# Output projection, second norm and gate logits: from single items among the score work to one TensorE piece per tile ahead of a value block

## What is computed

```
mod = silu(c) @ wmod                                   # six rows of 256 per batch
h = layernorm(x) * (1 + ca) + sa
x1 = x + ga * (softmax(causal(rope(q) @ rope(k).T / 4)) @ v  @ out_w + out_b)    # 16 heads of 16
h2 = layernorm(x1) * (1 + cb) + sb
logits = h2 @ gate_w.T;  top 4 of 16 experts (2 of 4 groups), weights from sigmoid(logits)
out = x1 + gb * (sum over the 4 experts of w * expert(h2) + shared(h2))          # SwiGLU, width 192
```

## Time and profile before

| | us |
|---|---|
| three runs, lowest / median / highest | 3317.51 / 3322.41 / 3326.74 |
| profiled execution: own time / span of the instructions | 3325.06 / 3323.3 |
| mean granted TensorE clock | 0.946 |
| first exponential of attention / end of the last one | 344 / 2234 |

### The profile page before, as it was taken

The page is one execution under the profiler, slowest core; times in us unless marked ns, Lnnn a source line. Parts: engine busy times, 40 slices in busy tenths (PEclk is TensorE's granted clock), DMA queues, the critical chain, the costliest instruction groups (busy, mean ns, idle before and its releaser), DMA issues.

```text
span 3323.3 us, 61013 instructions
## 1 busy us (share of the span) xinstructions
PE 2940.9 (88%) x22500; PEld 1617.6 (49%) x22500; DVE 2242.5 (67%) x5047; ACT 1782.1 (54%) x2736; POOL 1316.6 (40%) x1685
## 2 busy tenths in 40 slices
PE   7888699999999999899989878788877899999886
PEld 4433133334333334333333222227867788999775
DVE  7787398888888888999978656313921125555455
ACT  3322457666566665566555445565644555666222
POOL 6855111224422245221357556343045523441355
PEclk9989799999999999999989888899988999999898
DMA  4833513222322223212324433144355545664455
GB/s 163 207 108 94 113 40 63 61 66 67 86 62 54 54 69 102 49 31 60 76 92 125 108 88 95 54 135 140 93 166 164 169 136 163 178 183 139 143 175 152
DMA packets 290690, 359.05 MB, mean 108 GB/s; under 512 B 65404, under 2 KB 243212, under 8 KB 290140
## 3 DMA queue, kind: packets, MB, share of 16 engines
q1 hardware_dynamic: 259516, 279.94, 31.1%
q0 software_dynamic: 30208, 71.87, 7.2%
q10 hardware_dynamic: 672, 3.34, 0.4%
HBM read 206.25 MB, written 139.21 MB: 104 GB/s over the span
## 4 chain that ended last, share of the span: by engine, by line
PE 54%; DVE 11%; ACT 10%; issue 7%; another core or an unknown queue 3%; POOL 2%; DMA 1%; SPq 1%; DVEq 0%; ACTq 0%; POOLq 0%
PE PB L1140 13%; ACT P L1616 9%; PE PB L1067 9%; PE PB L1156 9%; DVE mx L1435 7%; PE PB L1014 6%; PE PB L1037 6%; PE PB L1050 5%; PE PB L1125 2%; PE PB L1081 2%; PE PB L1104 1%; POOL x_slots L1811 1%; PE PB L1017 0%; POOL P L1763 0%
## 5 line engine op out<-in xcount | busy, mean ns | idle before, releaser
L1435 DVE TENSOR_REDUCE mx<-PB 128x1 f32<-128x512 f32 (+3 forms) x2560 | 1405.7, 603 | 289.8 <-PE PB L1014 145.3
L1616 ACT ACTIVATE P<-PB 128x1024 f32<-128x1024 f32 (+3 forms) x1280 | 1100.0, 894 | 747.9 <-PE PB L1050 705.3
L1014 PE MATMUL PB<-KO,QO 64*128 64x512 bf16 (+3 forms) x2560 | 775.1, 358 | 80.9 <-DVE mx L1435 54.5
L1067 PE MATMUL PB<-P,V 128*17 128x512 f32 (+3 forms) x5120 | 610.5, 549 | 15.8 <-POOL P L1763 15.8
L1037 PE MATMUL PB<-QO,KO 64*128 64x512 bf16 (+3 forms) x2560 | 547.9, 358 | 56.4 <-ACT P L1616 30.6
L1050 PE MATMUL PB<-QO,KO 34*128 34x512 bf16 (+3 forms) x2560 | 539.0, 356 | 47.7 <-remote 38.3
L1014 PEld LDWEIGHTS PB<-KO,QO 64*128 64x128 bf16 x2560 | 203.8, 94 | 761.6 <-DVE mx L1435 542.7
L1546 DVE TENSOR_TENSOR haT<-sl,PB 64x128 f32<-64x128 f32 x350 | 101.5, 290 | 559.6 <-ACT sl L1695 383.2
L1140 PE MATMUL PB<-xT,ws 128*128 128x128 f32 x3432 | 446.6, 281 | 16.3 <-issue 9.6
L1763 POOL TENSOR_SCALAR_AFFINE_SELECT P<-P 128x256 f32<-128x256 f32 x512 | 207.5, 415 | 601.6 <-ACT P L1616 597.4
L1140 PEld LDWEIGHTS PB<-xT,ws 128*128 128x128 f32 x3432 | 420.3, 198 | 20.5 <-issue 11.7
(11 more groups left out here) (179 smaller groups left out, 3317.0 us busy)
## 6 DMA issues: line engine op xcount, KB each, us to landing
xq<-x_slots SPq DMA_DIRECT2D x286, 128.0 KB
qk_parts<-pt SPq DMA_DIRECT2D x192, 128.0 KB, 2.4
KO<-qk_parts SPq DMA_DIRECT2D x192, 128.0 KB, 3.9
y_slots<-yo SPq DMA_DIRECT2D x191, 128.0 KB
QO<-qk_parts SPq DMA_DIRECT2D x64, 256.0 KB, 3.6
rden<-rden_rows SPq DMA_DIRECT2D x256, 64.0 KB
y_slots<-mx SPq DMA_DIRECT2D x95, 128.0 KB
v_rows<-vst SPq DMA_DIRECT2D x16, 544.0 KB, 3.4
```

The source lines that it names most:

```text
L1014: mm = pe.matmul(PB[:, bank, 0:n], QO[half, k3, j, 128 * t:128 * t + 128], KO[half, k3, j, 512 * kc:512 * kc + n], start=True, stop=True)
L1067: mm = pe.matmul(PB[32 * j:32 * j + 17, 7, c0:512], V[:, g % 2, kt, 17 * j:17 * j + 17], P[:, pbuf(g, i, j // 2), j % 2, 0:n], start=kt == ...
L1435: dve.tensor_reduce(mx[:, j, t, kc:kc + 1], PB[:, u.bank[item], 0:n], AX.X, ALU.max).then_inc(s["mx"], 1)
L1616: act.activation(P[:, pbuf(g, i, p), :, 0:n], PB[:, 2 * p:2 * p + 2, 0:n], ACT.Exp, scale=0.25).then_inc(s["exp"], 1)
```

## The change

The tile's three TensorE parts (`o_logits` of tile it - 6, `o_turn` of tile it - 5, `o_proj` of tile it - 1) stand one behind another, ahead of the value block of a step. VectorE's parts of logits and projection become items of their own, `x_logits` and `x_proj`, placed right behind the three, ahead of the value block too. `o_h2` and `o_stat` follow in the same step, behind the exponential; `o_x1` and `o_load` at the same place of the next step. The rates count tiles: 0.3 a step in g % 4 == 3 (after a lead of 1), 0.48 in the two groups after it; a tile takes two steps at least, and credit goes on growing while a projection waits for "packed". In the expert stage the generator is pumped as before, five yields a job, but a tile has three yields now and had up to seven.

```diff
     def project(b):
-        stages = ("o_load", "o_proj", "o_x1", "o_stat", "o_h2", "o_turn", "o_logits")
-        for it in range(16 + len(stages) - 1):
-            for d in reversed(range(len(stages))):
+
+        for it in range(16 + 6):
+            while it - 1 in range(16) and not o.has("packed", b, 3, (it - 1) // 4):
+                yield "wait"
+            for d, name in ((6, "o_logits"), (5, "o_turn"), (1, "o_proj")):
                 if 0 <= it - d < 16:
-                    while stages[d] == "o_proj" and not o.has("packed", b, 3, (it - d) // 4):
-                        yield
-                    unit(stages[d], b, it - d)
-                    yield
+                    unit(name, b, it - d)
+            for d, name in ((6, "x_logits"), (1, "x_proj")):
+                if 0 <= it - d < 16:
+                    o(name, b, it - d)
+            yield "pe"
+            for d, name in ((4, "o_h2"), (3, "o_stat")):
+                if 0 <= it - d < 16:
+                    o(name, b, it - d)
+            yield "other"
+            for d, name in ((2, "o_x1"), (0, "o_load")):
+                if 0 <= it - d < 16:
+                    o(name, b, it - d)
+            yield "last"
 
     def route(p):
         o("route0", p)
-        while not o.has("o_logits", (FIRST[p] + TILES[p] - 1) // 16, 15):
+        while not o.has("x_logits", (FIRST[p] + TILES[p] - 1) // 16, 15):
             yield
...
-    pumps = []
+    pumps, tiles, stage = [], [], "last"
     for n, (g, i) in enumerate(order):
         if i == 0:
-            pumps = []
+            pumps, tiles = [], []
             if g % 4 in (0, 1) and g > 3:
-                pumps.append([proj[g // 4 - 1], 0.0, 2.5])
+                tiles = [proj[g // 4 - 1], 0.0, 0.48]
             if g % 4 == 3:
-                pumps.append([proj[g // 4], -8.0, 2])
+                tiles = [proj[g // 4], -1.0, 0.3]
             if g >= 8:
                 pumps.append([part0, 0.0, 0.7 if g == 12 else 1.7 if g > 12 else 1.4])
...
         if len(pend) == 2:
+            if tiles and i >= 2:
+                tiles[1] += tiles[2]
+                if tiles[1] >= 1 and stage != "other" and next(tiles[0], "done") == "pe":
+                    tiles[1] -= 1
+                    stage = "pe"
             values(*pend.pop(0))
...
         o("exp", g, i, 1)
+        if tiles and stage in ("pe", "other"):
+            stage = next(tiles[0])
         if i >= 2:
             pumped(pumps)
...
-                elif name == "o_proj":
+                elif name == "x_proj":
...
-                    dve.tensor_tensor(xo[:, i % 2], PB[:, u.bank[item], 0:256], obB[:, :], ALU.add).then_inc(s["xo"], 1)
+                    dve.tensor_tensor(xo[:, i % 2], PB[:, u.bank["o_proj", b, t], 0:256], obB[:, :], ALU.add).then_inc(s["xo"], 1)
...
-                elif name == "o_logits":
+                elif name == "x_logits":
...
-                    dve.tensor_copy(L[:, i, :], PB[:, u.bank[item], 0:16]).then_inc(s["L"], 1)
+                    dve.tensor_copy(L[:, i, :], PB[:, u.bank["o_logits", b, t], 0:16]).then_inc(s["L"], 1)
```

## The result

The changed kernel takes 3385.38 us (3379.1 to 3390.16, four runs) against 3319.96 us (3314.77 to 3326.74) of the kernel before beside it: 1.019 of its time, 95% interval 1.0171 to 1.0209. The profiled execution has a span of 3377.3 us, 54.0 over before. Forecast were 3344 and a range up to 3380: the direction is right, but the forecast rise of 21.5 us is a third of what came. The profiled execution of the changed kernel is the shortest of its four, and the one before was above its median, so the profiles show 54 of the 65 us between the medians.

The account below looks back on a forecast made before the run. TensorE bounds a plain step, with VectorE 0.3 us to spare; emptied VectorE decides at full pieces. 15 + 6.5 + 0 = +21.5 us on 3322.41 gives 3344; range 3332 to 3362 by batch bounds, 3292 to 3380 at 8 in 10.

Parts of the forecast that it names:

- What VectorE loses at a piece: Full pieces in attention: VectorE, without maxima to read for 2.28 us, makes a tile cost 2.85 us in place of 2.1.
- Batches 0 and 1: Groups 3, 4, 7 and 8: pieces sum to 41.4 us against 34, +7.4 a batch, +15 for both.
- the four with a projection alone: Tiles 0 to 3 of a batch, before any turn or logits: nothing drained, 1.05, 1.05, 1.5 and 1.9 us.
- the signs named beforehand: Groups 3, 4, 7, 8: VectorE's busy time unchanged, idle time up; projection wait short, first maximum's wait over 0.8 us.
- The five pieces without a projection: Last five pieces of a batch, only turn and logits: 0.62 us and a little each, 3.4 together.
- TensorE's price: Piece ahead of the value block: 1.49 us a tile on TensorE, between 1.3 and 1.96.
- The 1.2 us that spacing should have given back: Two full pieces in group 3, four steps apart at 0.3 tiles a step, give back 1.2 us a batch.
- the rival at 3295: TensorE's price alone decides, VectorE's window being hidden: tiles get 0.5 us cheaper, -27 us in all; chance 0.25.
- Batch 2: Groups 11 and 12: +5 in group 11, where VectorE has 0.07 us a step to spare, and 1.5 in group 12.
- The clock: Six projected groups of batches 0 to 2: granted clock falls by 0.04, 30 us more, 3374; chance 0.1.
- The expert stage: Batch 3's other eight tiles: turns wait at the end for GpSimd's four passes a tile, +3 us, between 0 and +8.
- Group 15: No maxima to read there, so eight tiles of batch 3 gain 0.5 us where all three parts are in, some -3.

Follow-up runs that it names:

- e5: The changed kernel again, unedited, on chip 13; 3147.18 us, 1.0171 of the kernel before.
- e2: The changed kernel with VectorE's maximum reading only the first quarter of each block of scores; 3256.77 us, 0.974 of the kernel before.
- e3: The changed kernel with logits and turn ahead of one step's value block, the projection ahead of the next one's; 3373.8 us, 1.0095 of the kernel before.
- e9: The changed kernel with the same three units in a row moved to mid-step, behind the exponential; 3117.39 us, 1.0086 of the kernel before.
- e6: The changed kernel with the two later groups' rate at 0.36 tiles a step in place of 0.48; 3133.65 us, 1.0132 of the kernel before.
- e1: The kernel before with VectorE's maximum reading only the first quarter of each block of scores; 3238.93 us, 0.9683 of the kernel before.
- e11: The kernel before again, unedited, for its profile on chip 15; 3093.85 us, one run.
- e12: e9 with an even pace (0.3 and 0.42 tiles a step, credit capped at 1.3) and the old expert pace; 3094.76 us, 1.0006 of the kernel before.
- e4: The changed kernel with only the expert stage's old pace of tiles put back; 3388.31 us, 1.0129 of the kernel before.

## Why the prediction was right and wrong

- **What VectorE loses at a piece: right.** Forecast were 2.85 us for a full piece, and 2.95 and 2.81 were measured in batches 0 and 1, by steps against group 5's. Both hold some time at the lower clock; e5's batch 0, where no full piece has any, gives 2.68. For the four with a projection alone, 5.5 in sum were forecast and 4.4 came; for the fifth 2.3 and 2.0. e2 shows that VectorE is the engine, e3 and e9 that run and place make the gap. Busy time unchanged and idle time up, the signs named beforehand, are in the profile. One sign was wrong: the wait for the projection was to stay short, and it is the larger half of the gap (1.00 and 0.88 us in the piece shown, 1.88 together for the 1.69 forecast).
- **Batches 0 and 1: 4 us each over the forecast.** The five pieces without a projection were put at 3.4 us by TensorE's price. They cost 6.3 in batch 0, some 1.5 of it by the lower clock, and 3.5 in e2: VectorE is the later engine there too (1.17 us of its work in a step). The 1.2 us that spacing should have given back didn't come (e6 shows that a plain step more gives nothing back). And the clock was counted at nothing: e5's groups 3 and 4, the same instructions, took 244.7 us in place of 247.7, with some 7 us less at the lower clock.
- **TensorE's price: too low.** 1.49 us came from rows among expert jobs, where all neighbours are full height in one column group. Ahead of the value block it was 1.68 (e2). Even so a full piece cost TensorE 1.4 to 1.7 us beyond the plain steps in e2, against 1.9 a tile in e1, not far from the 0.5 us gain that the rival at 3295 counted with. What failed in that rival is its condition, a hidden VectorE.
- **Batch 2: the failed step.** "24 against 127 - 108 = 19, +5; group 12 adds 1.5", bounds -6 and +14; it was +25.4. I took group 12 for a group 4. The runs show three things in its place. TensorE's waits for VectorE in groups 11 and 12 grew from 8 to 15 us: the same gap, dearer beside routing. With VectorE relieved 20 of the 25 go (e1, e2), and with the gap shortened likewise (e9 261.7 against e11's 256.9). The time at the lower clock grew from 17 to 34 us, worth some 7 us by the estimate below. And the scatter began in group 12, where TensorE stood 7.2 us for the mask; that is why group 12 alone grew by 18 us, but over both groups the waits for the mask grew by 1 us only. Counted by steps, a full piece cost 4.6 us in batch 2, but that includes 10 us of the first steps of group 12; without them it is nearer 3.7. How the rest of the 25 us divides stays open.
- **The clock: a rival that came true in part.** It had put a fall of 0.04 in the six projected groups at 30 us. The mean fall was 0.015. By an estimate from groups 4 and 8 of the changed kernel and of e5 (same instructions: 129.1 us with 10 at the lower clock and 126.1 with 3; 131.2 with 3 and 135.6 with 14), a microsecond there costs 0.4 us more. The six groups had 24 us at the lower clock before and 51 after, so some 11 of the 54 us are the clock's. Whether the clock follows the gap isn't shown: group 4 stayed at 1.00 in e3, e9 and e12, with the gap shortened, but also in e6 with the gap, and had 0.97 in e2 without it.
- **The expert stage: right mechanism, wrong size.** Forecast +3 (0 to +8), measured +9.3, and some 12 by e4. I had counted GpSimd's passes, but not that every turn waits for them in TensorE's own order: six waits of up to 2.7 us, 9.9 together, in the 50 us after 2330. In e3, with four yields a tile, the stage was no longer than at the old pace.
- **Group 15** was to gain 3 us by TensorE's price and lost 1; with 1.68 for 1.49 there was little to gain.
- **The range** ended 5 us short: +14 was the most that batch 2 was given, and +25 came. The narrower range of 3332 to 3362 doesn't follow from the bounds it names: those of batches 0 and 1 alone are -16 and +30.

## What to carry to other kernels

Where two engines hand buffers over in rotation, a run of units as long as the rotation empties the reader. What that costs depends on what else stands before the reader's next buffer. Price it as a gap of the reader: from its last read to its next one, with everything that the writer does in between. An engine with 67% busy over the span had 0.3 us a step to spare, and that decided. And a cost found beside plain work has to be worked out again for each stage in which another job already uses the slack. Before a long group is put down to one wait, list all its waits: in group 12 the longest was for a third engine.

## What the runs showed of the hardware

- The kernel before took 3320 us beside the first result, 3342 on chip 11, and 3090 to 3094 on chips 13, 15 and 7. Between its first profile and e11's, groups 1 to 8 agree to 1.5 us; the difference lies in the stages with indirect transfers, groups 13 and 14 (75 us) and the expert stage (150 us). Group 13 took 149 us with a DMA share of 0.39 and 106 GB/s in the first profile, and 104 with 0.54 and 149 GB/s in e11. The loss by the change was 1.9% and, on chip 13, 1.7%.
- TensorE's granted clock was below 1.00 in some groups where it was over 94% busy: 0.96 in group 4 of the changed kernel, 0.99 in e5's, with the same instructions (129.1 and 126.1 us). The longest idle stretch of it in the first was 0.6 us. In e9's group 4, as busy (115.83 of 120 us), the clock was 1.00. The Trainium skill (TensorE: Matmul & The Clock Gate, Why this matters for your kernels) warns of much longer gaps; this trace shows lower clocks without them.
